# Mixes for values and decays in a tile pair of their own, and all mixes ahead of both recurrences in five PSUM banks

## The reference, cut to what matters

```
xr_j = xn + sx * (maa_j + tanh((xn + sx*maa_x) @ maa_w1)_j @ maa_w2_j)      j = 0 (keys), 1 (decays), 2 (values), 3 (receptance), 4 (gate)
k = mix_0 @ Wk;  v = mix_2 @ Wv;  r = mix_3 @ Wr;  g = silu(mix_4 @ Wg)
w = exp(-exp(time_decay + tanh(mix_1 @ decay_w1) @ decay_w2))
state_t = w_t * state_(t-1) + k_t v_t;   y_t = r_t . state_(t-1) + bonus     (32 heads of 16 x 16)
out = groupnorm(y) * g @ Wo
```

## Time and profile before

| | |
|---|---|
| median of 3 runs | 3318.3 us (3316.11 to 3318.38) |
| the profiled execution's own time | 3324.42 us |
| its span | 3323.1 us |
| PE busy | 3102.3 us, 93% of the span |
| DVE, ACT, POOL busy | 41%, 34%, 30% |
| chain that ended last | PE 73%, DVE 7%, ACT 6%, POOL 6%, issue 4%, DMA 3% |

### The profile page before, as it was taken

How to read it: one execution, slowest core, us unless ns; L and a number is a source line. 1 busy time by engine, 2 the same in 40 slices (tenths; PEclk the granted TensorE clock), 3 DMA queues, 4 the chain that set the end, 5 groups by cost and what they waited for, 6 DMA issues and landing times.

```text
span 3323.1 us, 43816 instructions
## 1 busy us (share of the span) xinstructions
PE 3102.3 (93%) x16648; PEld 2589.2 (78%) x16648; DVE 1353.3 (41%) x3056; ACT 1115.1 (34%) x2492; POOL 1004.4 (30%) x938
## 2 busy tenths in 40 slices
PE   6988888999999999999999999999899989979988
PEld 3555556888888888889888888888688777758866
DVE  5784866333333333433333333334211455541133
ACT  2333335333222222332232222323333444443331
POOL 4564544222122121231121211212352232335410
PEclk8897989999999999999999999999899999979989
DMA  6554631332122121121121221211111101101132
GB/s 216 180 169 165 197 127 51 140 128 104 61 84 82 69 88 69 66 85 59 69 101 67 77 82 69 88 69 51 38 64 62 40 24 40 42 28 67 51 93 79
DMA packets 95095, 285.93 MB, mean 86 GB/s; under 512 B 8280, under 2 KB 52824, under 8 KB 86056
## 3 DMA queue, kind: packets, MB, share of 16 engines
q1 hardware_dynamic: 94408, 282.44, 24.9%
q10 hardware_dynamic: 480, 0.69, 0.1%
HBM read 260.94 MB, written 22.15 MB: 85 GB/s over the span
## 4 chain that ended last, share of the span: by engine, by line
PE 73%; DVE 7%; ACT 6%; POOL 6%; issue 4%; DMA 3%; SPq 0%; POOLq 0%; ACTq 0%; DVEq 0%
PE bank L179 21%; PE bank L180 20%; PE bank L181 20%; PE bank L1789 5%; POOL W_lo L219 3%; PE bank L1774 2%; DMA W_raw<-in_weights 1%; ACT W_hi L210 1%; DVE max L1982 1%; PE bank L2356 1%; DMA v_spread<-v_rows 1%; ACT prob L1871 1%; ACT prob L2467 1%; PE bank L633 1%; POOL y L1213 1%
## 5 line engine op out<-in xcount | busy, mean ns | idle before, releaser
L2063 POOL TENSOR_SCALAR prob<-prob,inverse 112x376 f32<-112x376 f32 x256 | 144.2, 584 | 1285.6 <-DVE inverse L1988 1285.6
L219 POOL TENSOR_TENSOR W_lo<-W_raw,W_hi 128x1024 fp32r<-128x1024 f32 x138 | 329.5, 2410 | 147.6 <-ACT W_hi L210 144.1
L179 PE MATMUL bank<-ctx_hi,W_hi 128*128 128x376 f32 x1024 | 353.2, 345 | 4.3 <-DVE K_lo L261 2.8
L180 PE MATMUL bank<-ctx_lo,W_hi 128*128 128x376 f32 x1024 | 343.0, 335 | 0.0
L181 PE MATMUL bank<-ctx_hi,W_lo 128*128 128x376 f32 x1024 | 342.4, 334 | 0.0
L261 DVE SCALAR_TENSOR_TENSOR K_lo<-bank,vectors,K_hi 128x375 fp32r<-128x375 f32 (+1 forms) x288 | 172.9, 606 | 413.3 <-ACT K_hi L252 413.3
L179 PE MATMUL bank<-act_hi,W_hi 128*128 128x448 f32 x800 | 319.5, 399 | 11.9 <-DVEq L338 5.6
L180 PE MATMUL bank<-act_lo,W_hi 128*128 128x448 f32 x800 | 299.1, 374 | 0.0
L181 PE MATMUL bank<-act_hi,W_lo 128*128 128x448 f32 x800 | 298.6, 373 | 0.0
L1935 DVE TENSOR_TENSOR V<-bank,bv 128x512 f32<-128x512 f32 x168 | 116.2, 692 | 437.6 <-PE bank L1789 236.6
L1871 ACT ACTIVATE prob<-bank,minus 112x376 f32<-112x376 f32 x256 | 143.6, 573 | 433.4 <-DVE minus L1985 433.4
(11 more groups left out here) (256 smaller groups left out, 6417.1 us busy)
## 6 DMA issues: line engine op xcount, KB each, us to landing
W_raw<-in_weights SPq DMA_DIRECT2D x69, 1024.0 KB, 4.9
ctx_hi<-ctx_split SPq DMA_DIRECT2D x64, 752.0 KB, 4.3
ctx_lo<-ctx_split SPq DMA_DIRECT2D x64, 752.0 KB, 5.8
v_spread<-v_rows SPq DMA_DIRECT2D x128, 224.0 KB
att<-in_ctxT SPq DMA_DIRECT2D x16, 376.0 KB, 5.2
ctx_split<-W_hi SPq DMA_DIRECT2D x16, 376.0 KB, 3.8
ctx_split<-W_lo SPq DMA_DIRECT2D x16, 376.0 KB, 4.7
W_hi<-ctx_split SPq DMA_DIRECT2D x32, 188.0 KB, 4.0
```

The costliest lines, as they stand in the source:

```text
L179: nc.tensor.matmul(dst, left[0], right[0], start=first, stop=False)
L180: nc.tensor.matmul(dst, left[0], right[1], start=False, stop=False)
L219: pool.tensor_tensor(k.Wl[:, slot, cs, :], k.Wraw[:, cs, :], k.Wh[:, slot, cs, :].bitcast(F32), ALU.subtract).then_inc(*k.w_low.now((n, i)))
L2063: pool.tensor_scalar(k.Pm[:, h, :], k.Pm[:, h, :], k.rsum[:, h:h + 1], 1.0, ALU.mult, ALU.mult).then_inc(*k.prob_done.now((n, h)))
```

## The change: what it does

It adds a tile pair `x2_hi`, `x2_lo` (slot 2) for the mixes of the values (j = 2) and, after them, of the decays (j = 1). The pair lies in the memory of `rT`, `state` and `tmp`, which the recurrence fills later; so in the second half the first mix waits for the last read of the first recurrence, and the first state tiles wait for the decays' product. The mix for keys is then free of the values' blocks, while that for decays waits for the last value block. The rotation has five banks (0, 1, 6, 2, 5), and PE issues two chunks of the mixes 0 and 1 behind each value block. After them come (in the second half) the output rows, then the decays, two chunks of mix 3, the first block of k, two more chunks of mix 3, `pe_decay_out`, and the first block of r. ACT, DVE, POOL and SP get orders to match: in the second half the weight of k is split ahead of the mix for decays, that of r between the chunks of mix 3, and POOL splits the context pieces 10 to 15 behind the weight of r. The weight slots and their order of loading (k ahead of r in the second half) go with it.

```diff
-MIX_SLOT = {2: 0, 0: 0, 1: 1, 3: 1, 4: 0}
+MIX_SLOT = {2: 2, 0: 0, 1: 2, 3: 1, 4: 0}
+MIX_BANKS = (0, 1, 6, 2, 5)
...
-        keys = [("mix", half, 2, c) for c in range(C)] + [("v", half, o) for o in range(C)]
-        keys += [("mix", half, 0, c) for c in range(C)] + [("mix", half, 1, c) for c in range(C)] + [("dec1", half)]
-        keys += [("mix", half, 3, c) for c in range(C)] + [("dec2", half, c) for c in range(C)]
-        keys += [("k", half, 0), ("r", half, 0)]
+        keys = [("mix", half, 2, c) for c in range(C)]
+        for o in range(C):
+            keys += [("v", half, o)] + [("mix", half, o // 2, 2 * (o % 2) + i) for i in range(2)]
+        keys += [("dec1", half), ("mix", half, 3, 0), ("mix", half, 3, 1), ("k", half, 0), ("mix", half, 3, 2), ("mix", half, 3, 3)]
+        keys += [("dec2", half, c) for c in range(C)] + [("r", half, 0)]
...
-        u.rotate(keys, [0, 1, 6])
+        u.rotate(keys, MIX_BANKS)
...
 def pe_rwkv(k):
...
+            if half and c == 3:
+                pe_centre(k, 0, C - 1)
+                pe.wait_ge(*k.scan_done[0, 63])
             pe_mix(k, half, 2, c)
...
-        for c in range(C):
-            pe_mix(k, half, 0, c)
+            for i in range(2):
+                pe_mix(k, half, o // 2, 2 * (o % 2) + i)
         if half:
             for i in range(HB):
                 pe_out_chunks(k, 0, i, range(C))
+        pe_decay(k, half)
+        pe_mix(k, half, 3, 0)
+        pe_mix(k, half, 3, 1)
         for c in range(C):
-            pe_mix(k, half, 1, c)
-        pe_decay(k, half)
-        for c in range(C):
-            pe_mix(k, half, 3, c)
+            pe_project(k, half, "k", 0, c)
+        pe_mix(k, half, 3, 2)
+        pe_mix(k, half, 3, 3)
         pe_decay_out(k, half)
...
-        for name in "kr":
-            for c in range(C):
-                pe_project(k, half, name, 0, c)
+        for c in range(C):
+            pe_project(k, half, "r", 0, c)
...
 def x_slot_free(half, j):
-    if j == 2:
+    if j == 0:
         return ("gate", half - 1, C - 1) if half else None
-    if j == 1:
+    if j == 3:
         return ("out", half - 1, HB - 1) if half else None
-    return {0: ("v", half, C - 1), 3: ("dec1", half), 4: ("k", half, C - 1)}[j]
+    return {2: None, 1: ("v", half, C - 1), 4: ("k", half, C - 1)}[j]
...
 def act_rwkv(k):
...
+        act_value_rows(k, half, 0)
         if half:
             act_root(k, 0, C - 1)
...
+        act_mix(k, half, 0, 0)
+        act_mix(k, half, 0, 1)
+        act_value_rows(k, half, 1)
+        act_mix(k, half, 0, 2)
+        act_mix(k, half, 0, 3)
+        if half:
+            act_gated(k, 0, C - 1)
+        act_value_rows(k, half, 2)
+        act_value_rows(k, half, 3)
+        act_split_weight(k, w["k" if half else "r"])
         for c in range(C):
             act_mix(k, half, 1, c)
...
+        act_mix(k, half, 3, 0)
+        act_mix(k, half, 3, 1)
+        if half:
+            act_split_weight(k, w["r"])
+        act_mix(k, half, 3, 2)
+        act_mix(k, half, 3, 3)
         if half == 0:
             act_split_weight(k, W_VALUES[0])
             act.wait_ge(k.rec_loaded, 48)
+        act_projected(k, half, "k", 0)
         act_decay(k, half)
         act_decay_to_bank(k, half, 0)
-        act_projected(k, half, "k", 0)
...
 def pool_rwkv(k):
...
         if half:
+            pool_split_weight(k, w["k"])
             pool_cx(k, 8)
             pool_cx(k, 9)
         pool_split_weight(k, w["r"])
-        if half:
-            pool_cx(k, 10)
-            pool_cx(k, 11)
-            pool_split_weight(k, w["k"])
-        for m in range(12 if half else 4, 8 * half + 8):
+        for m in range(10 if half else 4, 8 * half + 8):
             pool_cx(k, m)
...
+def mix_tiles(k, sb):
+
+    k.xh2, k.xl2 = sb("x2_hi", [P, C, HALF], F32R), sb("x2_lo", [P, C, HALF], F32R)
```

More of the change, by code:

```diff
@@ L60 @@
 MADE = 1
-ORDER = (["v", "k", "r", "v1_0", "g", "o", "v", "r", "k"] + [f"v1_{g}" for g in range(1, MADE)] + ["g", "o", "fr", "fk"]
+ORDER = (["v", "k", "r", "v1_0", "g", "o", "v", "k", "r"] + [f"v1_{g}" for g in range(1, MADE)] + ["g", "o", "fr", "fk"]
          + ["fv", "q1_0", "k1_0", "o1_0"] + [f"{w}1_{g}" for g in range(1, G) for w in ("qko" if g < MADE else "qkvo")] + UNIQUE[UNIQUE.index("q2_0"):])
@@ L481, in plan_rwkv @@
     for half in range(2):
[L482 to L485 removed]
+        keys = [("mix", half, 2, c) for c in range(C)]
[3 more added lines that the diff above has]
+        keys += [("dec2", half, c) for c in range(C)] + [("r", half, 0)]
         if half:
             tail(k, 0)
[L488 removed]
+        u.rotate(keys, MIX_BANKS)
+        for n, key in enumerate(keys):
+            k.last_mixed[half, MIX_BANKS[n % len(MIX_BANKS)]] = key
         u.rotate([(name, half, o) for name, o in LATE_KR], [0, 1])
@@ L541, in x_in_slot @@
 def x_in_slot(k, slot, c):
+    if slot == 2:
+        return k.xh2[:, c, :], k.xl2[:, c, :]
     cols = half_columns(slot)
@@ L803, in act_mix @@
         act.wait_ge(*k.banks.filled(x_slot_free(half, j)))
+    if c == 0 and half and j == 2:
+        act.wait_ge(*k.y_done[0, 63])
     xh, _ = x_in_slot(k, MIX_SLOT[j], c)
@@ L820, in act_projected @@
     act.wait_ge(*k.banks.filled(key))
+    if (name, o) == ("r", 0):
+        act.wait_ge(*k.banks.filled(("dec1", half)))
     act.copy(flat({"k": k.kT, "r": k.rT}[name][:, o]), k.banks.tile(key)[:, 0:HALF]).then_inc(*k.banks.draining(key))
@@ L826, in act_keys_to_bank @@
     act.wait_ge(*k.banks.drained(("k", half, o)))
+    if o == 0:
+        act.wait_ge(*k.banks.drained(k.last_mixed[half, KEY_BANK]))
     if o or half:
@@ L834, in act_decay_to_bank @@
     act.wait_ge(*k.decay_done[half, o])
+    if o == 0:
+        act.wait_ge(*k.banks.drained(k.last_mixed[half, DECAY_BANK]))
     if o or half:
@@ L845, in act_init @@
         act.wait_ge(*k.y_done[half, n - 4])
-    elif half:
-        act.wait_ge(*k.y_done[half - 1, 60 + n])
+    else:
+        act.wait_ge(*k.banks.filled(("dec1", half)))
     b0 = half * HB
@@ L901, in act_rwkv @@
             act_mix(k, half, 2, c)
-            if half and c == 1:
+            if half and c == 2:
                 act_square(k, 0, C - 1)
+        act_value_rows(k, half, 0)
         if half:
             act_root(k, 0, C - 1)
[L906 to L912, removed]
+        act_mix(k, half, 0, 0)
[8 more added lines that the diff above has]
+        act_split_weight(k, w["k" if half else "r"])
         for c in range(C):
             act_mix(k, half, 1, c)
-        if half:
-            act_split_weight(k, w["k"])
         key = ("dec1", half)
@@ L1018, in dve_mix_low @@
     xh, xl = x_in_slot(k, MIX_SLOT[j], c)
+    if c == 0 and half and j == 2:
+        dve.wait_ge(*k.y_done[0, 63])
     dve.wait_ge(*k.x5_high[half, j, c])
@@ L1036, in dve_outer @@
         dve.wait_ge(*k.y_done[half, n - 4])
-    elif half:
-        dve.wait_ge(*k.y_done[half - 1, 60 + n])
+    else:
+        dve.wait_ge(*k.banks.filled(("dec1", half)))
     if d == 0:
@@ L1138, in dve_rwkv @@
             dve_mix_low(k, half, 2, 3)
+            dve_mix(k, half, 0, 0)
             dve_variance(k, 0, C - 1)
+            dve_mix(k, half, 0, 1)
+            dve_mix_low(k, half, 0, 0)
             dve_scale(k, 0, C - 1)
             dve_gated(k, 0, C - 1)
+            dve_mix_low(k, half, 0, 1)
+            dve_mix(k, half, 0, 2)
+            dve_mix(k, half, 0, 3)
+            dve_mix_low(k, half, 0, 2)
+            dve_mix_low(k, half, 0, 3)
         else:
             dve_mixes(k, half, 2)
-        dve_mixes(k, half, 0)
+            dve_mixes(k, half, 0)
+        dve_mixes(k, half, 1)
         if half:
             dve_rwkv_out(k, 0)
-        dve_mixes(k, half, 1)
         dve_mixes(k, half, 3)
@@ L3197, in build @@
             shift_tiles(k, tiles(outer))
+            with ExitStack() as inner:
+                mix_tiles(k, tiles(inner))
             with ExitStack() as inner:
```

19 lines of the change are left out of this document (7 added, 12 removed).

## The result

The changed kernel takes 3328.3 us (median of 7 runs, 3323.3 to 3335.3) against 3318.4 (7 runs, 3316.1 to 3321.2) for the kernel before: ratio 1.0028, 95% interval 1.0018 to 1.0038, some 9.9 us slower. A second series gave 3325.5 (8 runs) against 3318.5 (30 runs), ratio 1.0021, 1.0011 to 1.0032. So it is slower by 0.2 to 0.3%. Its profiled execution took 3328.0 with a span of 3326.6.

The account below looks back on a forecast made before the run. A chain of handovers between PE, DVE and ACT, each letting PE's clock fall, was taken as the bound; 5.0 us gained in the first stage plus 1.2 in the second took 6.2 off 3318.3, giving 3312.1 us, range 3303 to 3324.

Parts of the forecast that it names:

- First stage, up to E: First half, to the end of the decays' product (E): 72.3 instead of 76.7, 4.4 us earlier.
- First stage, behind E: From the decays' product to the first recurrence's first read: 92.8 instead of 97.81, 5.0 us gained.
- SP's loads of weights swap places but not sizes: SP's order of weight loads: bounded by 0 and about 1 us, taken at 0.
- Second stage: Second half: decays' product 10.1 us earlier, but POOL's six context pieces, 22.1 us, keep the first read at 325.9.
- rival (c): Slower by POOL's queue behind the weight of r, once the decays' product ends after 293.9: 3326 us, chance 0.14.
- The 1.2 us of backlog: Second recurrence, step 6: SP issues its late load right behind the last context store, 1.2 us gained.
- Rival (a): PE's waits on drained banks go entirely and its clock stays up: 3305 us, chance 0.22.
- The signs that the prediction named: Trace marks of right or wrong: first read at 91 to 95, second-stage decays' product over by 296, among others.

Follow-up runs that it names:

- before_again: The kernel before, with no edit, run once more for a second trace: 3317.9 us, ratio 0.9995.
- after_again: The changed kernel, with no edit, run once more for a second trace: 3325.5 us, ratio 1.0021.
- ctx_first: The changed kernel, with SP's pass for context pieces 2 and 3 ahead of the value rows in the first half: 3319.5 us, ratio 1.0004.
- pieces_ahead: The changed kernel, with context pieces 10 and 11 ahead of the weight of r again on POOL: 3316.6 us, ratio 0.9994.
- both_orders: The changed kernel, with SP's context pass ahead of the value rows and POOL's pieces 10 and 11 ahead of r's weight: 3312.3 us, ratio 0.9984.
- before_g_late: The kernel before, with SP loading g's weight only after the first read in the first half: 3324.9 us, ratio 1.0014.
- g_behind: The changed kernel, with the load of g's weight behind three more spread loads in the first half: 3324.7 us, ratio 1.0018.
- before_pieces_behind: The kernel before, with context pieces 10 and 11 behind POOL's weight of k in the second half: 3319.0 us, ratio 1.0004.

## Why the prediction was wrong, step by step

**First stage, up to E: right in kind, too large in size.** The half clock in the first pair and the second block came as forecast. The last value block ended at 64.4 (forecast 62.3), E at 74.9 (72.3): the first block ended at 47.4, as before, and not at 46.5, and the pair behind the second block took 2.0 instead of 1.6. The gain of 4.4 at E was 1.8 against the trace that it was summed from, and nothing against before_again (74.7).

**First stage, behind E: the step that failed.** "POOL's context pieces and its last weight (4.65) come to an end at about 87 by the same sums, and POOL waits idle": they ended at 97.0. The sums followed PE, DVE and ACT only. The prediction had the last value block 7 us later and did not ask what SP had queued behind its rows: the loads that feed POOL. That moved the first read by about 1 us. The larger cost is the next one: "SP's loads of weights swap places but not sizes", taken at 0, missed that the load of g is released by POOL: while it waits, the spread load of step 4 waits behind it. Instead of 5.0 gained, read 63 is 4.5 us later in after_again than in before_again. ctx_first, which mends only SP's order, has 243.65 there against 243.10: with the queue mended the loss is gone, but the 5.0 do not appear. The term was mis-sized too. The six executions of edited versions of the changed kernel have read 0 at 95.0 to 95.9, the four of the kernel before and its edited versions at 95.7 to 97.8, which is 1.4 earlier by the means. The two halves of the failure are one chain: value rows, context loads, POOL's weight, g's load, spread load.

**Second stage: right in mechanism, wrong against what it was held.** E was to come 10.1 earlier by the way PE goes; the way was 9.4 shorter. POOL's queue was to take 22.1 behind the weight and took 22.7; ACT split the weight of r at E + 4.1, as forecast; the read started at E + 32.5 (rival (c) had E + 32.0). As the stage also began 5.9 late, read 64 was not at 325.9 but at 333.0. And "as before" was measured on an execution with the low clock, one of two levels that the four traces with this stage's old orders show: before_again reaches that read at 320.8. Against before_again's stage, 56.7 us from read 63 to E, the kernel after has 51.7, a gain of 5 and not of 10. Held against the first trace, the distance from read 63 to read 64 is a loss of 84.2 less 83.1, 1.1 us, near the forecast of nothing; held against before_again it is one of 84.5 less 77.7, 6.8. pieces_ahead, timed beside it, puts the price of the queue at 8.9 by medians. This is rival (c)'s mechanism; its condition, an E later than 293.9, was met, but by the late start from the first half and not by a low clock, so its price had a second way to come about, which the chance of 0.14 left out.

**The 1.2 us of backlog: wrong.** The load of step 6 goes out right behind SP's last store of context, at 333.98, 1.0 behind the first read, as forecast. But DVE could use its values only at 341.40, 7.4 us behind that issue and not 6.6 as in the earlier trace rows, so the step that had waited in the earlier trace rows starts 8.4 behind the first read, as before (8.5). What slowed the load is open.

**Rival (a), the rule on banks.** The mixes' waits on drained banks went from 11.4 us to nothing (the decays' products got one of 3.1 and one of 1.2), the clock in the first stage rose from 0.75 to 0.78, and the time rose. The Trainium skill, "Perfetto Trace Analysis", section "Matmul Optimizations", asks for all 8 banks in use and matmuls back to back. The change goes part of the way, with five banks for three. For PE the traces agree: the way to E is shorter in the second stage in every one of them. Whether it pays hangs on the other queues: 1.0028 with them as they were in the kernel after, 0.9984 in both_orders.

**The sum from medians.** From after_again: ctx_first gives 6.1 back and pieces_ahead 8.9, 15.0, of which 13.2 is found together. Without these two costs the change gains 5.9 by medians. That this is close to the forecast 6.2 is luck: the forecast had 5.0 of it in the first half and nothing at read 64, and the traces of both_orders and before_again show nothing at read 63 and 5.9 at read 64.

**The signs that the prediction named.** POOL's last piece ended right where the first read of the second recurrence starts, DVE's first three scans were over at 323.1, 9.9 us ahead of that read, and the half clock stood in the second value block: right. The first read at 97.01 instead of 91 to 95, and E at 300.5 instead of by 296: wrong. A time over 3322 was to mean an E later than 294, and so it was; the wait at step 4 was not among the signs.

## What to carry to other kernels

When an edit makes one producer later, follow each queue that waits for it in order to its end, the loads behind its stores above all: here a value block 9 us later cost a load 30 us on. Ask of a buffer's reload which engine frees it, and what the issuing queue holds behind that reload. And before a chain is summed from one execution, compare its time with the median: one that lies 6 us above it may carry its excess in the very stretch that is summed. Here a second trace moved the base of one term by 5 us.

## What the runs showed of the hardware

A spread load of 224 KB landed later when SP had issued a load of 1 MB 0.4 us ahead of it: DVE could use its values 103.85 - 97.48 = 6.4 us behind the issue in the kernel after and 104.99 - 98.59 = 6.4 in before_g_late, both times after a wait. With the large load 5.2 us ahead, in the kernel before, the product stood 100.69 - 95.33 = 5.4 behind the issue and did not wait. So the large load costs at least 1.0 us. The updates of the load's semaphore in the traces tell more: the 16th comes at 99.12 in the kernel before, 3.8 us behind the issue, at 96.32 in g_behind, 4.3 behind (92.05), and 6.4 behind in the two others, so it costs 2.1 to 2.6. That the two transfers share the DMA engines is the likely reason, which no run here took apart.

The granted clock of one stretch differs between executions of one kernel: 0.76 and 0.85 in the second stage of the kernel before, with 4.2 us between their E. Two kernels with the same orders in that stage, before_g_late and before_pieces_behind, have 0.77 and 0.81.
